# Attention: contexts divided with queries along the free axis, the row sums spread and sent back by DMA instead of transposes, and orders of their own for the second attention's slots

## The reference

```
# layer 0, feed-forward branch: convolution, then bidirectional attention, then a mixture of 8 experts
scores = einsum('bhqd,bhkd->bhqk', q, k) / sqrt(dh)
ctx = einsum('bhqk,bhkd->bhqd', softmax(scores), v)
# layer 1, attention branch: two causal attentions with the same k, v
ctx = causal_attn(q, k, v)
q2 = conv(ctx) + conv_b
ctx2 = causal_attn(q2, k, v)
out = ctx2 @ out_w.T + out_b
```

## Time and profile before

| | |
|---|---|
| median of 3 runs | 3461.34 us (3455.52 to 3463.75) |
| the profiled execution, its own time | 3481.77 us |
| its span, first to last instruction | 3480.0 us |
| busy: PE, DVE, ACT, POOL | 3216.7, 2559.9, 2087.3, 831.7 us |
| bidirectional attention, PE busy in 500 to 960 us | 448.6 of 460 us |
| layer 1, PE busy in 2200 to 3480 us | 1168.3 of 1280 us |

### The profile page before, as it was taken

The page is one execution under the profiler, slowest core; times in us unless marked ns, Lnnn a source line. Parts: engine busy times, 40 slices in busy tenths (PEclk is TensorE's granted clock), DMA queues, the critical chain, the costliest instruction groups (busy, mean ns, idle before and its releaser), DMA issues. The chain is left out here.

```text
span 3480.0 us, 80944 instructions
## 1 busy us (share of the span) xinstructions
PE 3216.7 (92%) x32139; PEld 1880.7 (54%) x32139; DVE 2559.9 (74%) x5088; ACT 2087.3 (60%) x4201; POOL 831.7 (24%) x756
## 2 busy tenths in 40 slices
PE   6887599999999899999999999789999999999998
PEld 5876233333333577777777777545555545444454
DVE  5876788888887376667667667677777777777774
ACT  6774188888888443434343434156667777776766
POOL 3321111111110242242242243223332211111110
PEclk8998799999999999999999999789999999999998
DMA  4100211111110001011011001222222121112110
GB/s 140 33 13 1 62 47 56 56 56 56 56 43 28 27 23 36 23 33 36 23 33 30 29 23 33 64 60 62 59 60 42 53 61 45 48 42 57 39 32 25
DMA packets 180487, 152.11 MB, mean 44 GB/s; under 512 B 44388, under 2 KB 160900, under 8 KB 179972
## 3 DMA queue, kind: packets, MB, share of 16 engines
q1 hardware_dynamic: 173092, 141.21, 14.4%
q0 software_dynamic: 6144, 4.72, 1.0%
q10 hardware_dynamic: 864, 0.79, 0.1%
HBM read 48.45 MB, written 32.65 MB: 23 GB/s over the span
## 5 line engine op out<-in xcount | busy, mean ns | idle before, releaser
L1461 DVE TENSOR_REDUCE b_maxima<-psum 128x2 f32<-128x1024 f32 (+3 forms) x768 | 774.4, 1045 | 239.0 <-PE psum L1260 215.3
L1401 ACT ACTIVATE b_prob<-psum 128x512 f32<-128x512 f32 (+2 forms) x1536 | 725.6, 526 | 329.0 <-PE psum L1293 299.9
L1461 DVE TENSOR_REDUCE c_maxima<-psum 128x2 f32<-128x1024 f32 x512 | 594.3, 1219 | 60.4 <-PE psum L1254 60.3
L1401 ACT ACTIVATE c_prob<-psum 128x512 f32<-128x512 f32 x1024 | 551.1, 597 | 121.6 <-PE psum L1286 101.2
L2213 PEld LDWEIGHTS psum<-consts_layer,a_hid 128*128 128x128 f32 x4096 | 476.2, 192 | 53.6 <-issue 53.3
L2203 PE MATMUL psum<-a_x1t,consts_layer 128*128 128x512 f32 x1024 | 464.0, 599 | 16.1 <-issue 10.5
L2213 PE MATMUL psum<-consts_layer,a_hid 128*128 128x128 f32 x4096 | 477.8, 274 | 0.0
L2273 ACT ACTIVATE a_hid<-psum,consts_layer 128x512 f32<-128x512 f32 x512 | 348.1, 687 | 211.0 <-PE psum L2203 205.1
L1286 PE MATMUL psum<-b_qa,b_ka 64*128 64x512 bf16 (+3 forms) x2048 | 365.5, 303 | 60.8 <-ACT b_prob L1401 56.5
L1317 PE MATMUL psum<-b_prob,b_v 128*32 128x512 f32 (+3 forms) x4096 | 387.6, 451 | 0.2
L2435 DVE SCALAR_TENSOR_TENSOR a_acc<-psum,a_gprob,a_acc 128x128 f32<-128x128 f32 x512 | 143.7, 343 | 270.4 <-PE psum L2213 258.4
(11 more groups left out here) (406 smaller groups left out, 4286.6 us busy)
## 6 DMA issues: line engine op xcount, KB each, us to landing
b_qa<-b_part SPq DMA_DIRECT2D x192, 128.0 KB
c_qa<-c_part SPq DMA_DIRECT2D x96, 128.0 KB, 2.4
b_ka<-b_part SPq DMA_DIRECT2D x96, 128.0 KB
c_ka<-c_part SPq DMA_DIRECT2D x90, 128.0 KB, 2.4
consts_layer<-layer_in SPq DMA_DIRECT2D x1, 5419.0 KB, 19.2
c_xt<-xnt SPq DMA_DIRECT2D x17, 256.0 KB, 2.8
m_xin<-x SPq DMA_DIRECT2D x16, 256.0 KB, 4.3
xnt<-m_xt SPq DMA_DIRECT2D x16, 256.0 KB, 2.7
```

The costliest lines, as they stand in the source:

```text
L1401: self.nc.scalar.activation(out, src, ACT.Exp, scale=SCALE).then_inc(self.s.free, 1)
L1461: self.nc.vector.reduce_max(out, src, X).then_inc(self.m.free, 1)
```

## The change

The transposes go (12 per turn), and with them both `vector_context` and the copy of `whole`. In their place the context stays with its queries along the free axis. For each pair SP sends the eight rows of sums (8 partitions of 512) spread over 128 partitions of 32, and the whole copy `c` to DRAM; VectorE inverts the 128x32; SP stores the inverse, waits for that, and loads it back with each head's row repeated over 8 partitions (`scale`), and the context's rows without gaps (`unscaled`). One product of 128x512, on GpSimd in the first stage and on VectorE in slot 6 (NORMALISE) in layer 1, makes the normalised context. The convolution, the output projection and the store of `ctxt` now wait for it.

In the causal attention each tile of a group has its own order of scores, jobs and values; the values' products of tile 1 stay where they were, those of tile 0 and 2 come in halves of their columns, and the convolutions and the output projection have other slots. The diff, cut:

```diff
-WHOLE = 3
+SPREAD = 16
...
-        self.rsum = sb("rsum", [P, T, 2 * HG])
-        self.ctxn = [sb(f"ctxn{n}", [P, T, D]) for n in range(2)]
+        self.spread = [sb(f"spread{n}", [P, S // SPREAD]) for n in range(PAIRS)]
+        self.unscaled = sb("unscaled", [P, S])
+        self.scale = sb("scale", [P, S])
...
-    def ended(self, p, s):
-
-        jobs = [(p - 1, PAIRS - 1)] if s == 1 else [(p, s // (2 * T) - 1)] if s > 2 * T and s % (2 * T) == 1 else []
+    def inverting(self, p, s):
+
+        early, late = (3, 15) if self.causal else (3, 14)
+        jobs = [(p - 1, PAIRS - 1)] if s == early else [(p, 0)] if s == late else []
...
+    def sync_spread(self, sp, p, pair):
+
+        heads = slice(pair * 2 * HG, (pair + 1) * 2 * HG)
+        sp.wait_ge(self.c_copied, p * PAIRS + pair + 1)
+        if p:
+            sp.wait_ge(self.normalised, p)
+        sums = self.c[pair][DH::GAP, :].rearrange("k (b x) -> k b x", b=SPREAD)
+        sp.dma_start(self.spread[pair][:, :], sums).then_inc(self.spread_loaded[pair], 16)
+        sp.dma_start(self.context_d[pair], self.c[pair][:, :]).then_inc(self.spread_loaded[pair], 16)
+
+    def sync_inverse(self, sp, p, pair):
+
+        heads = slice(pair * 2 * HG, (pair + 1) * 2 * HG)
+        rows = slice(pair * HALF, (pair + 1) * HALF)
+        sp.wait_ge(self.inverted, p * PAIRS + pair + 1)
+        sp.dma_start(self.inverse_d[heads, :].rearrange("k (b x) -> (k b) x", b=SPREAD), self.spread[pair][:, :]
+                     ).then_inc(self.inverse_stored[pair], 16)
+        sp.wait_ge(self.inverse_stored[pair], 16 * (p + 1))
+        inverse = self.inverse_d[heads, :].unsqueeze(1).broadcast_to([2 * HG, DH, S])
+        sp.dma_start(self.scale[rows, :], inverse).then_inc(self.scale_loaded[pair], 16)
+        sp.wait_ge(self.spread_loaded[pair], 32 * (p + 1))
+        context = self.context_d[pair].rearrange("(k x) q -> k x q", x=GAP)[:, 0:DH, :]
+        sp.dma_start(self.unscaled[rows, :], context).then_inc(self.scale_loaded[pair], 16)
+
+    def normalise(self, engine, compute, p, out):
+        for pair in range(PAIRS):
+            engine.wait_ge(self.scale_loaded[pair], 32 * (p + 1))
+        compute.tensor_tensor(out, self.unscaled[:, :], self.scale[:, :], ALU.mult).then_inc(self.normalised, 1)
...
-            if half == 0:
+            if half == int(self.causal):
...
-    def tensor_context(self, pe, p, pair):
-        out = self.m.bank("context", p, pair)
-        pe.wait_ge(self.c_copied, p * PAIRS + pair + 1)
-        pe.wait_ge(self.m.free, self.m.room("context", p, pair))
-        for t in range(T):
-            last = self.nc.tensor.transpose(out[:, 0, t * P:(t + 1) * P], self.c[pair % 2][:, t * P:(t + 1) * P], self.K("ident"))
-        last.then_inc(self.m.ready, 1)
-
-    def tensor_whole(self, pe, p):
-        out = self.s.bank("whole", p)
-        pe.wait_ge(self.m.free, self.m.count("context", p, PAIRS - 1))
-        pe.wait_ge(self.s.free, self.s.room("whole", p))
-        for t in range(T):
-            last = self.nc.tensor.transpose(out[:, t * P:(t + 1) * P], self.ctxn[p % 2][:, t, :], self.K("ident"))
-        last.then_inc(self.s.ready, 1)
...
             if self.causal:
-                scores(0)
-                maxima(0)
-                on_s()
-                scores(1)
-                on_m()
-                values(1)
-                maxima(1)
+                if t == 0:
+                    scores(0)
+                    maxima(0)
+                    on_s()
+                    on_m()
+                    scores(1)
+                    values(1)
+                    maxima(1)
+                elif t == 1:
+                    scores(0)
+                    maxima(0)
+                    on_s()
+                    values(1, 0)
+                    scores(1)
+                    on_m()
+                    values(1, 1)
+                    maxima(1)
+                elif t == 2:
+                    scores(0)
+                    maxima(0)
+                    on_m()
+                    on_s()
+                else:
+                    values(2)
+                    scores(0)
+                    maxima(0)
+                    on_s()
+                    values(1, 0)
+                    on_m()
+                    values(1, 1)
...
     def scalar_context(self, act, p, pair):
         act.wait_ge(self.pv_ready, p * SLOTS + (pair + 1) * 2 * T)
-        if p * PAIRS + pair >= 2:
-            act.wait_ge(self.m.free, self.m.count("context", *divmod(p * PAIRS + pair - 2, PAIRS)))
-        self.nc.scalar.activation(self.c[pair % 2][:, :], self.acc, ACT.Copy).then_inc(self.c_copied, 1)
+        if p:
+            act.wait_ge(self.spread_loaded[pair], 32 * p)
+        self.nc.scalar.activation(self.c[pair][:, :], self.acc, ACT.Copy).then_inc(self.c_copied, 1)
...
-    def vector_context(self, dve, p, pair, own):
-        nc = self.nc
-        dve.wait_ge(self.m.ready, self.m.count("context", p, pair))
-        if p * PAIRS + pair:
-            dve.wait_ge(self.m.free, self.m.count("context", *divmod(p * PAIRS + pair - 1, PAIRS)))
-        if pair == 0 and p >= 2:
-            dve.wait_ge(self.s.ready, self.s.count("whole", p - 2))
-        src = self.m.bank("context", p, pair)[:, 0, :].rearrange("p (t k x) -> p t k x", t=T, x=GAP)
-        own.done(nc.vector.reciprocal(self.rsum[:, :, :], src[:, :, :, DH]))
-        out = self.ctxn[p % 2][:, :, pair * 2 * HG * DH:(pair + 1) * 2 * HG * DH].rearrange("p t (k d) -> p t k d", d=DH)
-        nc.vector.tensor_tensor(out, src[:, :, :, 0:DH], self.rsum[:, :, :].unsqueeze(3).broadcast_to([P, T, 2 * HG, DH]), ALU.mult
-                                ).then_inc(self.m.free, 1)
+    def vector_inverse(self, dve, p, pair):
+        dve.wait_ge(self.spread_loaded[pair], 32 * (p + 1))
+        self.nc.vector.reciprocal(self.spread[pair][:, :], self.spread[pair][:, :]).then_inc(self.inverted, 1)
...
                 for p in range(-2, NB + 1):
                     if att.has(p):
                         att.sync_shift(sp, p, 1)
+                    if att.has(p - 1):
+                        att.sync_spread(sp, p - 1, PAIRS - 1)
                     if att.has(p + 2):
                         sp.wait_ge(att.s.free, att.s.count("conv", p + 2, 1))
                         sp.dma_start(xc_d[(p + 2) * P:(p + 3) * P, :], xc[:, :]).then_inc(xc_stored, 16)
                     if att.has(p + 4):
                         load_x(p + 4)
                     if att.has(p - 1):
-                        sp.wait_ge(att.s.free, att.s.count("whole", p - 1))
+                        att.sync_inverse(sp, p - 1, PAIRS - 1)
+                        sp.wait_ge(att.normalised, p)
                         sp.dma_start(ctxt_d[(p - 1) * P:p * P, :], ctxt[:, :]).then_inc(ctxt_stored, 16)
                     if att.has(p + 2):
                         att.sync_rows(sp, p + 2)
+                    if att.has(p):
+                        att.sync_spread(sp, p, 0)
                     if att.has(p + 1):
                         att.sync_shift(sp, p + 1, 0)
+                    if att.has(p):
+                        att.sync_inverse(sp, p, 0)
...
+                def normalise_context(p):
+                    if p:
+                        pool.wait_ge(ctxt_stored, 16 * p)
+                    att.normalise(pool, nc.gpsimd, p, ctxt[:, :])
+
+                for p in range(-1, LAST - 1):
+                    if att.has(p - 1):
+                        normalise_context(p - 1)
+                    att.pool_parts(pool, p + 2, att.s.count("k", p + 2))
+                normalise_context(LAST - 2)
...
-        QUERIES, KEYS, VALUES, CONVOLVE, OUTPUT = Front.QUERIES, Front.KEYS, Front.VALUES, (4, 8), 5
+        QUERIES, KEYS, VALUES, CONVOLVE, OUTPUT, NORMALISE = Front.QUERIES, Front.KEYS, Front.VALUES, (7, 9), 10, 6
...
                 for p in range(-1, len(turns) + 1):
+                    if att.has(p - 1):
+                        att.sync_spread(sp, p - 1, PAIRS - 1)
                     if att.has(p):
...
+                    if att.has(p - 1):
+                        att.sync_inverse(sp, p - 1, PAIRS - 1)
...
+                    if att.has(p):
+                        att.sync_spread(sp, p, 0)
+                        att.sync_inverse(sp, p, 0)
...
-                        pe.wait_ge(att.s.free, max(att.s.room("q", p + 2, n), att.s.count("whole", turn_of(b))))
+                        pe.wait_ge(att.s.free, att.s.room("q", p + 2, n))
+                        pe.wait_ge(att.normalised, turn_of(b) + 1)
...
-                        pe.wait_ge(att.s.free, att.s.count("whole", p - 1))
+                        pe.wait_ge(att.normalised, p)
...
+                def normalise_context(p):
+                    b = turns[p].batch
+                    if turns[p].first:
+                        if b >= 2:
+                            dve.wait_ge(att.s.ready, att.s.count("q", turns.index(seconds[b - 2]), 1))
```

(23 more changed lines are left out.)

32 lines of the change are left out of this document (15 added, 17 removed).

## The result

The changed kernel takes 3410.7 us (median of 4 runs, 3407.2 to 3415.3) against 3461.0 before: a ratio of 0.9857, 95% interval 0.984 to 0.9875, or 50 us less. The forecast was 3351, 110 us less. The profiled execution took 3415.3 us. The one of before lay 20 us above its own timed runs, so the two traces differ by 67 us.

A forecast was written before the change was run, and what follows sets the result against it. TensorE, 92% busy, was taken to set the pace in both stages. Gains of 34 us (bidirectional) and 88 (causal) less 12 at the ends, net 110, gave 3351 us; range 3305 to 3418.

The forecast's parts named there:

- Transposes, causal turns: Causal stage: twelve transposes fewer per turn save 1.75 us of TensorE's own time.
- Transposes, bidirectional turns: First stage: twelve transposes fewer plus 0.35 us of waits behind them save 2.1 us a turn, 34 us in 16.
- Orders: Causal slots: half of the values' products ahead of the second unit's scores fills holes, about 0.9 us a turn.
- Slots of the jobs: Causal turns: values' projection, shifts, output projection and convolution change slot, gaining 0.5 us a turn, bounds 0 and 1.
- VectorE's swap: VectorE trades two divisions for two reciprocals and a causal product (0.69 us), ScalarE loses a copy: counted as nothing.
- The chain: DMA chain of sums, inverses and context, the only new wait: charged 0.25 us a turn, bounds 0 and 2.
- Routed turns: Eight causal turns with routed experts' work: 2.3 us gained each, 18 us in all.
- Ends: Uncovered chain costs 4.4 us at the first stage's end, 5.4 at the kernel's end, 2 at first loads.
- The rivals: Besides late chain: more than counted 3306 (0.13), VectorE sets the pace 3385 (0.05), slower 3511 (0.06), no effect 3461 (0.02).
- the late chain: Each DMA leg lands 1 us later, VectorE waits some 2 us a turn in 32 turns: 3415 us, chance 0.14.
- The sum's own range: Whole kernel: 3325 to 3385 us around the likeliest 3351, chance 0.60.
- the signs named: Bidirectional turns 43.4 us, causal 32 to 33; against: VectorE idle over 1 us behind a DMA, bidirectional turns still 45.

The follow-up runs named there:

- e6: Kernel before with the new causal orders, convolution moved to slots 7 and 9 and output to slot 10, transposes kept: ratio 0.9966.
- product at 9: Changed kernel with VectorE's product of a second turn's context at slot 9 instead of 6: 3393.9 us, ratio 0.9802; again on another chip, 0.9834.
- e17: Kernel with product at slot 9 and convolution at 8 and 9, plus the first attention's values' product of a pair's first slot halved: ratio 0.9781.
- e1: Kernel before with only the new orders of TensorE's work within the causal slots: 3436.3 us against 3462.8, ratio 0.9925.
- e9: Kernel with product at slot 9, with the convolution's halves at slots 8 and 9 instead of 7 and 9: 3415.4 us against 3426.1.
- e3: Changed kernel with VectorE's product of a second turn's context at slot 9 instead of 6: 3393.9 us, ratio 0.9802.
- e4: Changed kernel with the causal stage's reciprocals and product reading a tile no DMA writes, so VectorE waits for no DMA there: 3400.8 us, ratio 0.9821.
- e7: Kernel with product at slot 9, without the DMAs of contexts, sums and inverses and without reciprocals, in both attentions: ratio 0.9728.
- e2: Changed kernel with the old order of the causal slots: 3419.0 us, ratio 0.9878.
- e12: The kernel with product at slot 9 run again, on another chip: 3426.1 us, ratio 0.9834.

## Why the forecast missed, point by point

**Transposes, causal turns: right.** 1.75 us was counted. From e6 to the product at 9, slots 1, 2, 3, 9 and 10 of a C turn lose 0.19, 0.40, 0.59, 0.18 and 0.40: 1.76.

**Transposes, bidirectional turns: mis-sized.** 2.1 counted, 1.3 measured. Slot 3 gave 0.57 as its row said, slots 1 and 9 0.31 and 0.42, though each lost 0.58 of work. The text held that nothing covers this time and added 0.35 for waits behind it. The waits ran the other way: in slots 1 and 9 the transposes filled time that TensorE otherwise waits for ScalarE (0.59 us), since the product with the values stands there in one piece behind the scores (e17). 16 us.

**Orders: right in sign, sized somewhat too large.** 0.9 counted, 0.6 measured (e1: 0.46 and 0.75), 7 us over 24 turns. The holes in the second slots went, as forecast: the second unit's two score matmuls, split in the earlier trace rows, stand together again (at 2882.10 in the changed kernel). The price is slot 2's, as the text feared, behind the product that stands whole in slot 1.

**Slots of the jobs: a step that failed.** +0.5 was counted, with 0 as the lower bound; alone they cost 0.5 (e6). The text said that the convolution leaves a slot where it covers a hole for one where it covers none, and did not price that. It priced only gains. In the changed kernel C still pays its 0.5, which e9 won back; P has got its part back with the transposes (the output costs 1.09 again). So the mean is -0.25, 0.75 off, 18 us.

**VectorE's swap: the other step that failed.** It was charged nothing, since "they wait for TensorE anyway". That holds for its busy time, but not for one long operation ahead of maxima that TensorE needs. The duration (0.69) was read from an operation with an input in PSUM, with GpSimd idle. Beside GpSimd's parts the product takes up to 2.2, and the maxima wait behind it. Slot 8 of P shows 1.6 us of it, 0.8 in the mean over both kinds: 19 us. e3 won 17 back. Only the turns with parts in slots 5 to 8 pay it.

**The chain: charged 0.25, cost 0.1 to 0.3** (e4, e7). The loads landed late enough for waits, and VectorE's slack took most of them. The Trainium skill ("DMA: Bandwidth & Descriptors", section "Why a DMA increments its semaphore by 16 and not by 1") would have these transfers use eight DMA engines. No run here tests that, and none contradicts it: at the end a load of 128 KB lands 3.6 us after its issue began (3403.34 to 3406.94), where one of 256 KB on 128 partitions took 3.2. It decided nothing.

**Routed turns: 18 counted**, 31 by the two traces, about 17 by the estimate for one chip.

**Ends: right.** 12 counted; the traces give 1 at the start, 4 between the stages (within what one kernel varies there) and 6 at the end, whose chain is, in the columns of the earlier trace rows:

```profile
3397.38 0.60 ACT L1446 ACTIVATE b_c<-psum 128x512 f32<-128x512 f32 x1 [0.55 <-PE psum L1353]
...
3400.89 0.35 DVE L1512 RECIPROCAL b_spread<-b_spread 128x32 f32<-128x32 f32 x1 [11.40 <-DMA b_context<-b_c]
...
3406.94 0.69 DVE L1260 TENSOR_TENSOR b_ctxt<-b_unscaled,b_scale 128x512 f32<-128x512 f32 x1 [5.69 <-DMA b_unscaled<-b_context]
3407.68 2.08 PE L2960 MATMUL psum<-consts_layer,b_ctxt 128*128 128x128 f32 x8 [10.37 <-DVE b_ctxt L1260]
```

9.7 us from the copy's end to the output, where it was 3.4.

**Sum.** Of the 60 us that are missing, 18 are the slots, 19 the collision, 7 the orders and 16 the first stage: 60. The chain's charge, a little too high, gives back up to 3, and the routed turns take 1. The shares are those along one path of edits (orders, slots, transposes, product); along another they shift, as e2 shows for the orders. Two slips of the text weigh nothing: four times 0.4 and 0.45 is 3.4 and not 3.6, so its upper bound for the orders was 2.6, and the first stage's end adds up to 1155.6. The granted clock of the earlier trace rows also falls to 0.7 once more (slice 26, ahead of the causal stage).

**The rivals.** None came true. The time of the late chain (3415) was nearly hit, by luck: the causes are others, and e4 and e7 rule its own out. The sum's own range (3325 to 3385) misses the measured time; the wide one holds it only by the room for that rival. Of the signs named, VectorE's waits for DMAs came and cost little, and the bidirectional turns stopped at 44.2 instead of 43.4.

## What to carry to other kernels

A removed instruction is worth its time only where nothing else waits at that place; look for the wait that it stood in before it is counted, and put a half of the next work there. A job moved from a slot in which other engines are busy to one in which they are not is priced with its whole duration. Before an elementwise operation with two inputs in SBUF goes to VectorE, look at what GpSimd does in that slot.

## What was not expected of the hardware

The same kernel (product at 9) took 3393.9 us on one chip (e3) and 3426.1 on another (e12), and the kernel before 3462.8 and 3483.6. Each chip was used in one session only, so chip and session can't be told apart. The eight routed turns of the two, with the columns of the earlier trace rows, and two lines of the second one's waits; first e3:

```profile
2295.75:2605.33 309.58, 294.31 (x4893) 172.57 (x4887) 253.44 (x325) 227.31 (x504) 123.52 (x129) 0.99 0.40 93
```

and e12:

```profile
2305.46:2643.27 337.81, 308.49 (x4895) 177.82 (x4891) 252.34 (x326) 227.22 (x504) 122.21 (x129) 0.98 0.37 86
```

```profile
DVE b_maxima L1498 <- remote: 19.2, 7, 4.7
ACT b_prob L1440 <- remote: 17.7, 6, 4.6
```

VectorE and ScalarE stand still for 19 and 18 us, up to 4.7 at a time, with a releaser outside the program's own events ("remote"). No trace from the two chips where before takes 3461 to 3463 has these lines. All from the three where it takes 3481 to 3486 have them, and so has the first profile of before (VectorE 15.3 us, ScalarE 2.2). Busy times are the same but for TensorE's (294.31 and 308.49), whose ends are modelled. What holds them up stays open. So a profile of before and one of after may be of different chips, and 20 to 30 us of their difference are then not the change's.
